# A macaron transformer block on one core: zeroing the staging areas at the start, on DVE and POOL

## The reference

```python
def ffn(x, g1, b1_, w1, b1, g2, b2_, w2, b2):
    h = layer_norm(x, g1, b1_)
    h = h @ ternary_quant(w1).T + b1             # 128 -> 512
    h = gelu(h)                                  # exact
    h = layer_norm(h, g2, b2_)
    return h @ ternary_quant(w2).T + b2          # 512 -> 128

x = x + 0.5 * ffn(norm(x))
x = x + attention(norm(x))                       # 16 heads of 8, relative positions
x = x + 0.5 * ffn(norm(x))
```

## Time and profile before

| | before |
|---|---|
| median of 3 runs | 461.84 us (460.36 to 462.55) |
| the profiled execution | 462.41 us |
| its span, first to last instruction | 460.6 us |
| DVE busy | 396.7 us, 86% |
| PE busy | 346.2 us, 75% |
| ACT busy | 262.2 us, 57% |
| POOL busy | 115.7 us, 25% |
| mean granted clock of TensorE | 0.933 of full |

### The profile page before, as it was taken

The page is one execution under the profiler, slowest core; times in us unless marked ns, Lnnn a source line. Parts: engine busy times, 40 slices in busy tenths (PEclk is TensorE's granted clock), DMA queues, the critical chain, the costliest instruction groups (busy, mean ns, idle before and its releaser), DMA issues.

```text
span 460.6 us, 17086 instructions
## 1 busy us (share of the span) xinstructions
PE 346.2 (75%) x6846; PEld 276.5 (60%) x6846; DVE 396.7 (86%) x569; ACT 262.2 (57%) x646; POOL 115.7 (25%) x158
## 2 busy tenths in 40 slices
PE   0877887063398987988988988889889889667784
PEld 0546664051176776766776767767667767663564
DVE  4979887146399999999999999999999999939685
ACT  1575544022566666666666666666666666613981
POOL 6574754200242012022021020120220210024652
PEclk9989988678589999999999999999999999977998
DMA  7004247899532132132231320321322301400002
GB/s 211 0 2 152 78 145 248 272 171 178 94 67 75 27 81 72 34 84 56 43 78 39 64 74 17 91 65 26 83 59 40 83 9 31 65 19 1 1 23 70
DMA packets 68627, 34.88 MB, mean 76 GB/s; under 512 B 37136, under 2 KB 67376, under 8 KB 68464
## 3 DMA queue, kind: packets, MB, share of 16 engines
q1 hardware_dynamic: 67824, 33.42, 30.4%
q10 hardware_dynamic: 576, 0.80, 0.7%
q0 software_dynamic: 192, 0.18, 0.2%
HBM read 19.17 MB, written 11.01 MB: 66 GB/s over the span
## 4 chain that ended last, share of the span: by engine, by line
DVE 57%; issue 17%; SPq 7%; ACT 6%; PE 5%; DMA 3%; POOL 3%; DVEq 1%; POOLq 0%; ACTq 0%
DVE pT L896 28%; DVE negmax L886 17%; SPq L353 4%; DVE xh L705 3%; DMA v_rep<-pT 2%; ACT v_rep L601 2%; ACT v_rep L589 1%; DVE stat L695 1%; PE pair L1169 1%; DMA x<-in_x 1%; PE pair L971 1%; DVE sqsum L814 1%; DVE x L828 1%; POOL grs L465 1%; DVE v_rep L820 1%
## 5 line engine op out<-in xcount | busy, mean ns | idle before, releaser
L628 ACT ACTIVATE probs<-pair,negmax 128x512 f32<-128x512 f32 x256 | 173.9, 684 | 116.7 <-DVE negmax L886 116.6
L896 DVE STREAM_TRANSPOSE pT<-probs 128x1024 f32<-128x1024 f32 x128 | 158.7, 1240 | 12.4 <-ACT probs L628 12.4
L886 DVE TENSOR_REDUCE negmax<-pair 128x2 f32<-128x1024 f32 x128 | 153.7, 1200 | 16.3 <-PE pair L1119 16.1
L1102 PE MATMUL pair<-stage_k,stage_c 128*32 128x512 f16 x1024 | 117.4, 408 | 67.0 <-ACT probs L628 51.2
L1108 PE MATMUL pair<-stage_z,stage_q 128*32 128x512 f16 x1024 | 111.9, 386 | 0.0
L1102 PEld LDWEIGHTS pair<-stage_k,stage_c 128*32 128x32 f16 x1024 | 50.6, 140 | 89.7 <-ACT probs L628 66.9
L1119 PE MATMUL pair<-stage_z,stage_q 128*32 128x222 f16 (+57 forms) x1024 | 103.3, 282 | 0.0
L511 POOL COPY v_diag<-v_rep 32x512 f32 (+1 forms) x60 | 36.6, 610 | 250.3 <-PE pair L1134 208.1
L1114 PE MATMUL pair<-stage_z,stage_q 128*32 128x16 f16 (+56 forms) x1024 | 98.7, 278 | 0.0
L1134 PE MATMUL pair<-pT,v_diag 128*32 128x128 f32 (+1 forms) x2176 | 92.6, 269 | 3.6 <-DVE pT L896 3.6
L1134 PEld LDWEIGHTS pair<-pT,v_diag 128*32 128x32 f32 x2176 | 72.6, 112 | 4.0 <-DVE pT L896 3.8
(11 more groups left out here) (108 smaller groups left out, 303.6 us busy)
## 6 DMA issues: line engine op xcount, KB each, us to landing
v_rep<-pT SPq DMA_DIRECT2D x16, 256.0 KB, 7.4
stage_z<-z_scratch SPq DMA_DIRECT2D x16, 254.0 KB
qs_scratch<-pT SPq DMA_DIRECT2D x12, 256.0 KB, 2.7
stage_q<-qs_scratch SPq DMA_DIRECT2D x126, 24.0 KB
stage_z<-z_scratch SPq DMA_DIRECT2D x16, 128.0 KB
qc_scratch<-pT SPq DMA_DIRECT2D x8, 256.0 KB, 3.0
kc_scratch<-pT SPq DMA_DIRECT2D x8, 256.0 KB, 3.2
stage_k<-kc_scratch SPq DMA_DIRECT2D x16, 128.0 KB
```

Source lines behind the costliest of these rows:

```text
L628: nc.scalar.activation(probs[:, q % 6, :], score_pair(q // 2)[:, q % 2, :], ACT.Exp, bias=negmax[:, q % 8:q % 8 + 1], accum_out=rowsum[:, ...
L886: nc.vector.tensor_reduce(negmax[:, 2 * n % 8:2 * n % 8 + 2], score_pair(n)[:, :, :], AX.X, ALU.max, negate=True).then_inc(max_ready, 1)
L896: nc.vector.transpose(pT[:, par, 2 * n:2 * n + 2, :].rearrange("p a s -> p (a s)"), probs[:, 2 * n % 6:2 * n % 6 + 2, :].rearrange("p a s ...
L1102: mm(bank[32 * j:32 * j + 32, :], all_rows[:, 32 * j:32 * j + 32], stage_k[:, par, :], start=True, stop=False, skip_group_check=True)
```

## The change

Eight memsets cover `stage_q` and `stage_c`, and two cover `v_diag`, as before. Of `stage_q`, five parts are now zeroed by DVE ahead of its first statistics, and the sixth by POOL. POOL does both halves of `stage_c`, that sixth part and half 0 of `v_diag` at its start, behind the zeroing of `zs`. Half 1 of `v_diag` is zeroed by POOL behind `ffn(0)` and the six loads that it issues. No POOL memset is left between the steps of the first FFN. The waits and their counts are unchanged.

```diff
             nc.gpsimd.memset(zs[:, :, :].bitcast(U32), 0).then_inc(zs_zero, 1)
-            nc.gpsimd.memset(stage_c[:, 0, :].bitcast(U32), 0).then_inc(stage_zero, 1)
+            for par in range(2):
+                nc.gpsimd.memset(stage_c[:, par, :].bitcast(U32), 0).then_inc(stage_zero, 1)
+            nc.gpsimd.memset(stage_q[:, 1, 2, :].bitcast(U32), 0).then_inc(stage_zero, 1)
+            nc.gpsimd.memset(v_diag[:, 0, :, :, :], 0.0).then_inc(v_diag_zero, 1)
...
-                    if n == 0:
-                        zero_stage(1, 0)
-                        zero_stage(1, 1)
-                    if n == 3:
-                        zero_stage(1, 2)
-                        zero_stage(1, 3)
-                    if n in (5, 9):
-                        nc.gpsimd.memset(v_diag[:, n // 9, :, :, :], 0.0).then_inc(v_diag_zero, 1)
...
             ln_rstd(0, 0)
-            for n in range(3):
-                zero_stage(0, n)
             ln_low(0, 0)
...
+            nc.gpsimd.memset(v_diag[:, 1, :, :, :], 0.0).then_inc(v_diag_zero, 1)
             pool.wait_ge(v_diag_zero, 2)
             pool.wait_ge(v_rep_in, 16 * 16)
...
+            for par, n in ((0, 0), (0, 1), (0, 2), (1, 0), (1, 1)):
+                nc.vector.memset(stage_q[:, par, n, :].bitcast(U32), 0).then_inc(stage_zero, 1)
 
             ln_stats(0, 0)
```

More of the change, by code:

```diff
@@ L434, in ln_low @@
                     .then_inc(s["xT_low"], 1)
-            def zero_stage(par, n):
-                if n == 3:
-                    nc.gpsimd.memset(stage_c[:, par, :].bitcast(U32), 0).then_inc(stage_zero, 1)
-                else:
-                    nc.gpsimd.memset(stage_q[:, par, n, :].bitcast(U32), 0).then_inc(stage_zero, 1)
             def ffn(f):
```

## The result

The changed kernel takes 457.84 us, median of ten runs, beside 461.70 us of ten runs of the kernel before: ratio 0.9901, 95% interval 0.9880 to 0.9922. The ratio is an estimate from all runs and not the quotient of the medians (0.9916): the medians are 3.9 us apart, the ratio makes it 4.6 (3.6 to 5.5). The same kernel was timed once more with the experiments, six runs beside 17 of before: 456.34 us and 463.21 us, ratio 0.9845, interval 0.9813 to 0.9876, or 7.2 us (5.7 to 8.7). The two intervals don't meet, so an interval understates by how much a repeated timing of the same two kernels can differ: here by 2.6 us. Between them lies what both pairs of profiles show at the end of the first FFN, about 5 us. The profiled execution took 458.05 us with a span of 456.3, against 462.41 and 460.6.

The account below looks back on a forecast made before the run. DVE holds 57% of the chain that ended last, and POOL counts only where DVE waits behind it. Gains build from 2.0 to 4.0 us by the second new `x`, all carried: 461.84 - 4.0 = 457.8 us, range 455.8 to 460.9.

Parts of the forecast that it names:

- POOL's start, nothing: Zeroing added at POOL's start, 3.62 us, fits into 3.79 us of idle time before the first `rs`, so costs nothing.
- DVE's start, 0.2 us late: Five memsets ahead of DVE's first statistics, priced at up to 1.24 us each, end at 6.55, 0.2 us late.
- A: First `xh`: 3.30 us becomes 1.10, less 0.2 of lateness; gain 2.0 us.
- B: Second `xh`: 2.04 us becomes 1.10, but the 0.94 us are hidden because TensorE comes later; gain stays 2.0.
- C: 29 to 36 us: POOL's reads move up and collide with DVE's sum; TensorE gains only 1.5 us, DVE 3.3.
- D: First new `x`: starts at 39.4 to 39.5 instead of 42.65, POOL's root ready by then; gain 3.2 us.
- E: Second new `x`: starts at 48.1 instead of 52.03, without the 1.80 us memset ahead of the root; gain 4.0 us.
- Behind the FFN, all of it kept: From `v_rep`'s issues through the attention loops to the end, the same work starts earlier; all 4.0 us carried.
- rival 1: Half the gain is hidden: moved-up POOL reads cost what the memsets cost, only A holds; 459.8 us, chance 0.13.
- rivals 2 and 3: DVE's start memsets and POOL's exclude each other: as doubled operations 460.8 us (0.07), at one element a step 464.4 (0.05).
- rival 4: The gain is absorbed behind the FFN by the stretch of transfers; 461.8 us, chance 0.06.
- `v_diag`, half 1, nothing: Half 1's 1.80 us, moved behind POOL's DMA issues, costs nothing: POOL stood idle 35.13 us before its copies.

## Why the prediction was right, and where not

The forecast was 457.8 us and 457.84 was measured. That they agree so closely is luck: the second timing gives 7.2 us less than before and not 4.0, and the spans of the two pairs of profiles 4.3 and 2.9. What can be judged is the sum, step by step, in the two pairs of the table.

- *POOL's start, nothing:* right to 0.1 us. POOL's memsets end at 7.33, and `rs` starts at 7.42, 0.19 us behind DVE's statistics and not 0.09 as before. That hardly any cover was left is what the kernel with all of them on POOL paid for.
- *DVE's start, 0.2 us late:* the price was wrong, and the thing that it was held against isn't fixed. The transpose's 1.24 us was the wrong neighbour; a memset starts every 1.075 us, as the Trainium skill's one cycle per element has it (page "VectorE: DVE Perf Modes", section "Zero memsets can be issued as uint32", estimate 1.07 us). The first began at 1.02, not 0.7, and the statistics start at 6.15, 0.83 us behind the start of the last one, the same distance as with three more memsets (8.54 and 9.37). In the eight profiles in which the statistics wait for the tokens they begin at 5.69 to 6.56, so the five memsets cost between nothing and 0.5 us, by execution.
- *That DVE's memsets don't hold POOL's:* right, and with it the rule of the Trainium skill, page "SBUF — State Buffer", section "Who interferes with whom". POOL's memsets at 2.85 to 7.33 are as long as alone. With copies in their place they are not.
- *A, 2.0 us:* 2.2 alone, in the timing and in the length of the `xh`. They end 2.4 us earlier in the first pair (12.23, 9.87) and 1.6 in the second (11.57, 9.96); the tokens make the difference.
- *B, hidden:* right; TensorE takes up the second group's tiles at 16.24 without a gap.
- *C, 1.5 us:* 2.5 in the first pair, 1.4 in the second. The mechanism held: POOL's reads now hold the sum (1.61 us) and the cast (1.38), as foretold. In the first pair the sum began at 26.71, not at 27.5. Of these 0.8 us, 0.3 are the lateness that wasn't there and the tokens; 0.4 come from the sum ahead of the third `xh`, which met less of the first group's constant on POOL (below); 0.2 from TensorE's clock (last section).

That sum before, and after:

```profile
24.61 1.21 DVE L814 TENSOR_TENSOR sqsum<-sqsum,v_rep 128x512 f32<-128x512 f32 x1 [0.58 <-ACT v_rep L601]
```

```profile
22.34 0.84 DVE L804 TENSOR_TENSOR sqsum<-sqsum,v_rep 128x512 f32<-128x512 f32 x1 [0.89 <-ACT v_rep L588]
```

- *D, 3.2 us:* 4.1 and 3.0. ScalarE's square came at 35.29 instead of 37.76, 2.5 us earlier: it rides on TensorE as said. POOL's root was not ready ahead of DVE, though: the new `x` waited 0.20 us for `grs`.
- *E, 4.0 us:* 5.1 and 4.0 (52.03 less 48.1 is 3.9, rounded up there). The 0.8 us that E was to add measured 1.0 and 1.1.
- *Behind E, the queues as before:* from the second new `x` to `v_rep` the changed kernel takes 39.9 us twice, the kernel before 40.1 and 40.9, so another 0.2 and 1.0 us are gained that the sum doesn't have. What differs there wasn't looked into.
- *Behind the FFN, all of it kept:* 0.9 and 0.5 us less at the first copy into `v_diag`; open, as told above.
- *The signs and the rivals:* a sum of squares over 1.5 us was to speak for rival 1, and there is one (1.61), but its 2.0 us lie outside both intervals. C had counted on the collision as well, so the length of that sum couldn't tell the two apart. POOL's memsets kept their length (rivals 2 and 3), and 4.4 and 4.5 us of gain are left behind the transfers (rival 4).
- *`v_diag`, half 1, nothing:* right. It runs at 83.68, and POOL is idle for 34.09 us behind it.

## What to carry to other kernels

- Before work is moved off an engine's queue, look at what takes its place beside the other engine: here a memset that only wrote was harmless to the neighbour's sums, and the read that moved up was not (1.46 us for 0.69), so that taking 1.8 us off POOL gained nothing.
- Work that nothing waits for belongs where its engine waits for a load, but only as long as the room is: 3.6 us fitted into 3.8, 8.2 did not.
- An operation that the trace doesn't show lies between its neighbours in it: here 1.075 us, between 0.95 and 1.24. Where an arrival varies by 0.9 us between executions, as that of the tokens does, a forecast of 0.2 us late means little.
- Take a second profile of both kernels before a step is explained by its gain: at the first new `x` the two pairs gave 4.1 and 3.0 us.

## What the runs showed of the hardware

**DVE and POOL share something that some operations need whole.** The engines do not meet at semaphores alone. Held by a POOL memset: `xh` (3.30 us for 1.11; the first of the four alone 2.73, beside POOL's three memsets of together 2.74), the cast (1.44 for 0.43), copies (5.79 us for four, while POOL's memsets took 6.77 us for 4.60). Not held: a sum of two tensors (0.69 us beside a memset), a DVE memset (1.075 us from start to start, with and without a POOL memset beside it). Held by a POOL operation that reads: sums too (1.46 us).

**TensorE's granted clock can fall at different places in two executions of one kernel.** Two profiles of the kernel before, in windows of 5 us, columns as above:

```profile
26.00:31.00 5.00, 4.87 (x22) 3.73 (x23) 3.37 (x14) 3.58 (x6) 2.92 (x4) 0.66 0.00 0
31.00:36.00 5.00, 3.91 (x38) 3.21 (x37) 4.96 (x7) 3.13 (x6) 4.39 (x4) 1.00 0.01 3
```

```profile
26.00:31.00 5.00, 3.54 (x24) 2.58 (x23) 3.48 (x11) 4.66 (x8) 3.85 (x5) 1.00 0.00 0
31.00:36.00 5.00, 3.96 (x26) 3.54 (x27) 4.96 (x9) 1.80 (x3) 3.45 (x3) 0.66 0.01 3
```

and the changed kernel:

```profile
26.00:31.00 5.00, 2.32 (x22) 1.64 (x21) 4.22 (x6) 5.00 (x9) 3.44 (x3) 1.00 0.00 0
31.00:36.00 5.00, 5.00 (x42) 4.53 (x40) 4.24 (x16) 2.81 (x6) 0.53 (x1) 1.00 0.31 113
```

The two levels are 1.2 and 2.4 GHz, so 0.66 of full over 5 us is 3.4 us at the lower one. In the first profile the fall lies at 26 to 31, in the second at 31 to 36, in the changed kernel at neither: there it comes at 39.7 to 43 us, in both of its profiles. What it costs depends on who waits for TensorE then: 0.2 us here (from the third `xh` to the sum of squares 3.77 us before, 3.61 after), some 2 us in the kernel with the copies, whose first new `x` began 10.4 us after the end of the split (32.88 to 43.31) and not 8.1 (30.45 to 38.57). The 2 us are an estimate from that one distance: from there on both kernels have the same instructions, and the clock is what differs between their windows.
